# First batch of a fused attention and expert kernel: row products of two pairs of heads in two passes, memory cleared elsewhere, new slot tables

## The reference

```python
x = x + xattn(_layernorm(x), ctx, ctx, ...)          # stage A, first half
n1 = _ln(_layernorm(x), ln1_g, ln1_b)                 # stage A, second half
q, kk, v = n1 @ wq + bq, n1 @ wk + bk, n1 @ wv + bv   # two blocks, 16 heads, 16 columns a head
attn = softmax(q @ kk.T / sqrt(16)); ctx = attn @ v   # 512 x 512 scores for each of 32 heads
x = x + mix(ctx @ wo)                                 # stage C
x = x + sum over top 2 experts of gate * (gelu(n2 @ fw1[e]) @ fw2[e])
```

## Time and profile before

| | |
|---|---|
| median of 3 runs | 1400.85 us |
| lowest, highest | 1398.68, 1401.18 us |
| the profiled execution, its own time | 1400.36 us |
| its span in the trace | 1398.6 us |
| PE, DVE, ACT, POOL busy | 1353.3, 1090.8, 885.8, 371.5 us |
| mean granted TensorE clock | 0.994 |

### The profile page before, as it was taken

How to read it: one execution, slowest core, us unless ns; L and a number is a source line. 1 busy time by engine, 2 the same in 40 slices (tenths; PEclk the granted TensorE clock), 3 DMA queues, 4 the chain that set the end, 5 groups by cost and what they waited for, 6 DMA issues and landing times.

```text
span 1398.6 us, 25195 instructions
## 1 busy us (share of the span) xinstructions
PE 1353.3 (97%) x8671; PEld 639.5 (46%) x8672; DVE 1090.8 (78%) x2368; ACT 885.8 (63%) x1693; POOL 371.5 (27%) x360
## 2 busy tenths in 40 slices
PE   7889999999999999999999999999999999999999
PEld 4633433455344543445444453445434454443356
DVE  6769987978789777987779787897879877787621
ACT  3256667775677656775577756776567755756751
POOL 8613151113413033223142133130332231330000
PEclk9999999999999999999999999999999999999999
DMA  4013012211311213211132103112131211212002
GB/s 118 17 46 99 24 58 88 77 54 31 107 66 66 69 39 114 76 62 47 46 114 77 54 31 106 63 70 69 39 114 69 68 48 46 84 47 69 17 1 90
DMA packets 90711, 90.34 MB, mean 65 GB/s; under 512 B 14880, under 2 KB 85664, under 8 KB 89692
## 3 DMA queue, kind: packets, MB, share of 16 engines
q1 hardware_dynamic: 90588, 88.73, 19.3%
HBM read 35.05 MB, written 4.25 MB: 28 GB/s over the span
## 4 chain that ended last, share of the span: by engine, by line
PE 79%; issue 8%; DVE 6%; ACT 5%; POOL 1%; DVEq 0%; ACTq 0%; POOLq 0%
PE psum L913 15%; PE psum L930 13%; PE psum L744 8%; PE psum L881 8%; PE psum L897 7%; PE psum L862 7%; PE psum L500 6%; PE psum L529 4%; DVE mx L1433 3%; PE psum L779 2%; ACT prob L1745 2%; PE psum L617 2%; PE psum L590 1%; PE psum L627 1%; PE psum L505 1%
## 5 line engine op out<-in xcount | busy, mean ns | idle before, releaser
L1745 ACT ACTIVATE prob<-psum 128x512 f32<-128x512 f32 x1024 | 555.3, 605 | 314.3 <-PE psum L930 206.4
L1433 DVE TENSOR_REDUCE mx<-psum 128x1 f32<-128x512 f32 x1024 | 642.6, 681 | 81.0 <-PE psum L897 78.7
L913 PE MATMUL psum<-qst,kst 64*128 64x512 bf16 x2048 | 296.2, 379 | 7.0 <-ACT prob L1745 3.8
L930 PE MATMUL psum<-prob,vst 128*17 128x512 f32 x2048 | 246.0, 595 | 0.6 <-ACT prob L1745 0.2
L897 PE MATMUL psum<-kst,qst 64*128 64x512 bf16 x1024 | 184.3, 379 | 9.9 <-DVE mx L1433 4.0
L913 PEld LDWEIGHTS psum<-qst,kst 64*128 64x128 bf16 x2048 | 75.8, 95 | 184.2 <-issue 136.4
L1896 POOL CAST parts<-resid 128x512 bf16<-128x512 f32 x64 | 40.8, 638 | 326.0 <-DVE resid L1304 326.0
L897 PEld LDWEIGHTS psum<-kst,qst 64*128 64x128 bf16 x1024 | 53.0, 93 | 142.6 <-issue 94.9
L881 PE MATMUL psum<-w,cxT 128*128 128x256 f32 x448 | 110.3, 393 | 0.0
L862 PE MATMUL psum<-n2T,x 128*128 128x512 f32 x224 | 103.2, 603 | 0.0
L930 PEld LDWEIGHTS psum<-prob,vst 128*17 128x17 f32 x2048 | 46.1, 96 | 122.4 <-issue 92.9
(11 more groups left out here) (251 smaller groups left out, 1703.2 us busy)
## 6 DMA issues: line engine op xcount, KB each, us to landing
kst<-parts SPq DMA_DIRECT2D x186, 128.0 KB, 2.1
qst<-parts SPq DMA_DIRECT2D x186, 128.0 KB, 2.1
cmat<-G_dram SPq DMA_DIRECT2D x7, 1024.0 KB, 4.6
x<-in_L_ffn_fw SPq DMA_DIRECT2D x14, 512.0 KB, 3.7
w<-in_L_ffn_fw SPq DMA_DIRECT2D x14, 512.0 KB, 3.8
xbuf<-in_x SPq DMA_DIRECT2D x8, 512.0 KB, 4.9
kin<-in_ctx SPq DMA_DIRECT2D x8, 512.0 KB, 4.0
out<-acc SPq DMA_DIRECT2D x7, 512.0 KB, 3.2
```

The costliest lines, as they stand in the source:

```text
L913: ins = e.matmul(psum[:, u.bank, :], kst[own, i, h // 2, g * P:(g + 1) * P], qst[own, i, h // 2, :], start=i == 0, stop=i == 1)
L930: ins = e.matmul(psum[32 * j:32 * j + VW, VB, :], vst[:, g, h, :], prob[:, g % 2, j, :], start=g == 0, stop=g == NT - 1, tile_position=(0, ...
L1433: e.tensor_reduce(mx[:, qq, par, j, t:t + 1], psum[:, u.bank, :], AX, ALU.max).then_inc(u.free, 1)
L1745: e.activation(prob[:, g % 2, j, :], psum[:, u.bank, :], ACT.Exp).then_inc(u.free, 1)
```

## The change

Five edits belong to the head of the program.

- The layers 1 of `kst` and `qst` are cleared only behind the first four head pairs (12 of 16 blocks), both by DVE: `kst` behind the gate columns, `qst` between `lf` and `F`. POOL clears only `chosen`.
- The products for pairs 0 and 1 go in two passes: first layer 0 of both (`pick_first`, high and middle part), later layer 1 (`pick_low`, high and low part), behind the third maximum tile.
- POOL makes both middle parts before both low parts.
- The projection of piece 2 (`p2`) moves from behind the last maximum's tiles to the slot of the last one. Pairs 2 and 3 come later between the maxima.
- `warm_clock(6)` becomes `keep_clock(4)`: four products of 256 columns in float32 in place of six of 512 columns in a one-pass format.

The slot tables of all three kinds of period are new. Only a few of their rows are shown.

```diff
-            PE_A=slots(-8, "kT0:4 kT1:0 qT0:0 qT1:0 gates:3 gsum:22 ...
+            PE_A=slots(-8, "kT0:4 kT1:0 qT0:0 qT1:0 gates:4 gsum:22 ...
...
-        HEAD = defaultdict(lambda: -9, p0=-7, s0=-7, p1=-6, s1=-6, pick2=3, pick3=9, p2=TILES, mean=TILES,
+        HEAD = defaultdict(lambda: -9, p0=-7, s0=-7, p1=-6, s1=-6, low=5, pick2=9, pick3=11, p2=TILES - 1, mean=TILES,
                            logits=TILES + 1, mexp=TILES + 1, s2=TILES + 1)
...
                         pick_first()
+                        yield "low"
+                        pick_low()
                         for h in range(PAIRS, HP):
                             yield f"pick{h}"
-                            pick([(which, j, h) for which in range(2) for j in range(3)])
+                            for which in range(2):
+                                for i in range(2):
+                                    pick(which, h, i)
...
             def pick_first():
 
-                for which, h in ((0, 0), (1, 0), (0, 1), (1, 1)):
-                    for j, made in enumerate((split_hi, split_mid, split_lo)):
-                        e.wait_ge(made, which + 1)
-                        pick([(which, j, h)])
+                for h in range(PAIRS):
+                    for which in range(2):
+                        e.wait_ge(split_hi, which + 1)
+                        e.wait_ge(split_mid, which + 1)
+                        pick(which, h, 0)
+
+            def pick_low():
+
+                for h in range(PAIRS):
+                    for which in range(2):
+                        e.wait_ge(split_lo, which + 1)
+                        pick(which, h, 1)
...
-            warm_clock(6)
+            keep_clock(4)
...
                 e.scalar_tensor_tensor(out=lf, in0=gf, scalar=0.0, in1=ga, op0=ALU.min, op1=ALU.subtract
                                        ).then_inc(va.here("lf", b), 1)
+                if b == 0:
+                    e.memset(qst[:, 1, HP:], 0.0).then_inc(ones, 1)
                 yield "F"
...
                     ins.then_inc(gate_setup, 1)
+                e.memset(kst[:, 1, HP:], 0.0).then_inc(ones, 1)
...
             e.memset(mrow[:], 1.0).then_inc(ones, 1)
-            e.memset(kst[:, 1], 0.0).then_inc(ones, 1)
...
                     yield f"s{n}"
-                    middle_low(b, n)
+                    if b == 0 and n < 2:
+                        middle(b, n)
+                        for k in range(2 if n else 0):
+                            low_part(b, k)
+                    else:
+                        middle_low(b, n)
...
             e.memset(vst[:, :, :, KD:KD + 1], 1.0).then_inc(consts, 1)
-            e.memset(qst[:, 1], 0.0)
             e.memset(chosen, 0.0).then_inc(choice_made, 1)
```

More of the change, by code:

```diff
@@ L370, in build @@
[L370 to L374 removed]
+            PE_A=slots(4, "kT0:2 kT1:3 qT0:2 qT1:0 gates:2 gsum:16 cols:17 cd0 cd1:0 st0:2 st1:0 st2:6 num0:3 num1:5 "
+                          "num2:0 num3:20 n1T0:0 n1T1:2 p0:5 p1:2 p2:9 p3:0 pv0:26 pv1:0 logits"),
@@ new lines, in build @@
+            ACT_S=slots(5, "p4:2 p5:16 p6:0 p7:14 v0:17 v1"),
+            POOL_A=slots(5, "pw:21 vcopy:10 mask0:9 mask1:3 mask2:0 mask3:0 vw:16 hw:11 hs:18 hn:0 x2:22 r1 r5:0 s0:0 "
+                            "s1:0 s2:9 s3"),
+            POOL_C=slots(22, "acc0:0 r1"),
+            POOL_S=slots(19, "s4:2 s5:6 s6:25 s7"),
+            SP_A=slots(-1, "ctx:0 x:2 gi:21 G:65 s0:3 s1:17 s2 s3"),
+            SP_C=slots(56, "w10:0 w20:7 w11:11 w21:24 out"),
+            SP_S=slots(-1, "s4:2 s5:24 s6:26 s7"),
@@ L505, in keep_clock @@
                     e.matmul(psum[:, VB, 0:2 * P], ident[:], ident[:].unsqueeze(1).to_broadcast([P, 2, P]), start=True,
-                             stop=True)
-            def warm_clock(n):
-                for _ in range(n):
-                    e.matmul(psum[:, VB, 0:4 * P], identR, identR.unsqueeze(1).to_broadcast([P, 4, P]), start=True,
                              stop=True)
@@ L679, in router, with pick @@
                 logits(u, mbc, rw, M)
-            def pick(order):
-                for which, j, h in order:
-                    for i in range(2):
-                        if j not in PARTS[i]:
-                            continue
-                        u = uses["pick", which, h, i] if j else take("pick", which, h, i)
-                        ins = e.matmul(psum[:, u.bank, :], chosen[:, which, i, PARTS[i].index(j), h, :], parts[:, which, j, :],
-                                       start=j == 0, stop=j > 0)
-                        if j:
-                            ins.then_inc(u.full, 1)
-            def pick_first():
-                for which, h in ((0, 0), (1, 0), (0, 1), (1, 1)):
-                    for j, made in enumerate((split_hi, split_mid, split_lo)):
-                        e.wait_ge(made, which + 1)
-                        pick([(which, j, h)])
+            def pick(which, h, i):
+                u = take("pick", which, h, i)
+                for n, j in enumerate(PARTS[i]):
+                    ins = e.matmul(psum[:, u.bank, :], chosen[:, which, i, PARTS[i].index(j), h, :], parts[:, which, j, :],
+                                   start=n == 0, stop=n == 1)
+                ins.then_inc(u.full, 1)
+            def pick_first():
+                for h in range(PAIRS):
[8 more added lines that the diff above has]
+                        pick(which, h, 1)
             def spread_G(b, h):
@@ L891, in maximum @@
                     for which in range(2):
-                        for i in range(2):
-                            w = uses["pick", which, h // 2, i]
-                            e.wait_ge(w.free, w.n)
+                        w = uses["pick", which, h // 2, 0]
+                        e.wait_ge(w.free, w.n)
                 for par, u in enumerate([take("max", b, qq, j, t, par) for par in range(2)]):
@@ L908, in score @@
                     e.wait_ge(rows_in[q_ % 2], 16 * (q_ // 2 + 1))
+                if b == 0 and h < HC and g == 0:
+                    for which in range(2):
+                        w = uses["pick", which, h // 2, 1]
+                        e.wait_ge(w.free, w.n)
                 us = [take("score", b, qq, g, 2 * j + par) for par in range(2)]
@@ L1194, in stage_a @@
                     residue(b, n)
-                for i in range(0 if b else 2):
-                    u = uses["pick", 1, 0, i]
+                if b == 0:
+                    u = uses["pick", 1, 0, 0]
                     e.wait_ge(u.full, u.n)
-                    e.tensor_copy(qst[:, i, 0, :], psum[:, u.bank, :]).then_inc(u.free, 1)
+                    e.tensor_copy(qst[:, 0, 0, :], psum[:, u.bank, :]).then_inc(u.free, 1)
                 yield "mean"
@@ L1888, in first_half, with middle @@
                 spread(b, slice(NG // 2, NG), 1)
-            def middle_low(b, n):
-                m, which, c = PIECES[n]
+            def middle(b, n):
                 q_, u = b * len(PIECES) + n, uses["proj", b, n]
@@ L1899, in middle_low @@
                                 ).then_inc(split_lo, 1)
+            def middle_low(b, n):
+                middle(b, n)
+                low_part(b, n)
             def second_half(b):
```

122 lines of the change are left out of this document (59 added, 63 removed), and 12 rows, old and new, of the table DVE_A.

## The result

| | before | changed |
|---|---|---|
| median, of 13 runs each | 1400.98 us | 1405.39 us |
| lowest, highest | 1398.68, 1402.99 us | 1402.7, 1407.6 us |
| ratio of the changed to before | | 1.003, 95% interval 1.0022 to 1.0039 |
| the profiled execution, its own time | 1400.36 us | 1406.88 us |
| its span | 1398.6 us | 1405.2 us |

The account below looks back on a forecast made before the run. TensorE, with work in flight for 97% of the span, was taken as the bound. Start -2.0, picks -1.5 and last maximum to first score -4.5 gave -8.0 us: 1392.9 us on the median's scale, range 1387.8 to 1397.6.

Parts of the forecast that it names:

- The lock on the port: Start: without POOL's qst memset blocking DVE's variance line, the first gate product moves from 12.83 to at most 8.8: 4.0 us.
- The clock of the gate products: Start: with little idle time in front, the gate products' 3.25 us pair may run at 2.4 GHz: 1.3 us won.
- The rival on the clock: Start: idle time before the first transpositions grows to 2.4 us, clock falls; start -0.3, total 1394.6 us; chance 0.15 within forecast's.
- The memset between `lf` and `F`: Start: DVE's new qst memset delays F, g, G and M, with nothing hiding it: 2.6 us lost.
- I charge 0.7 for both risks: Start: 0.7 us off the 2.7 us gain at G, for POOL's key-weight folding and a TensorE clock drop behind G.
- POOL's fold: Start: POOL folds the key weights until 29.8 us, unmoved by the change; a gain above 2.9 us would be cut off.
- The picks: Head: POOL's earlier middle part lets DVE's sixteen reductions start 2.1 us earlier; taken as -1.5 us, bounds 0.5 and 2.4.
- From the last maximum to the first score: Head: p2 and the gate sum leave this stretch, and the clock is fuller: -4.5 us, bounds 3.3 and 6.
- The first period: 91.6 to 242 us: 11.5 us open, but the trace doesn't say which order wins them: 0, with +-2 us.
- The middle periods: Six periods with 1.1 us each open to reordering: 0 with a fraction of that, so 163.5 us each.
- the late fourth pair behind `make_x3`: Middle periods: POOL's late parts make TensorE wait behind one maximum each; at 2 us each, 1404.9 us; chance 0.04.
- single pieces shifted by a few slots: Slot tables: changes move single pieces slightly; maxima placed by any slot differ by one at most in first and middle tables.

Follow-up runs that it names:

- the late clearing: Changed kernel with the qst memset behind M instead of between lf and F: 1400.67 us, ratio 1.0011; with all three old tables too, 1393.57 us, ratio 0.9949.
- 26 filling products: Changed kernel's head with all three old tables and keep_clock(26) instead of keep_clock(20) ahead of TensorE's wait for G: 1393.13 us, ratio 0.9953.
- the version with the lowest time: Changed kernel's head with qst cleared behind M, new first table, middle and last tables of before: 1390.73 us, ratio 0.9941.

## Why the prediction was wrong

By its own steps, each against what the profiles measured. The forecast was -8.0 us; the spans gave +6.6. The difference of 14.6 is 3.9 at the start, 0.9 at the picks, -0.3 at the first score, 1.4 in the first period, 2.65 in the middle ones, 1.1 from there to the ending and 5.0 in it.

- **The lock on the port, 4.0 us at the first gate product: right.** 12.83 became 8.78, at the late end of what was forecast. The memset of `kst` cost nothing, as taken: `lf` still waited 0.30 us for ScalarE behind it.
- **The clock of the gate products, 1.3: right.** L715's four took 1.91 instead of 3.25 us. Not always, though: in two other profiles with this head they took 2.84 and 3.06. The rival on the clock had put the four `keep_clock` products at 1.8 us by rows at the full clock; they took 3.78, and the first transpositions 0.6 more than before. So a part of that rival came true, but not by the growing idle time that it named.
- **The memset between `lf` and `F`, 2.6: right** in itself (2.62), and so was G at 25.4.
- **"I charge 0.7 for both risks": this step failed.** The clock drop behind G cost 10.28 - 5.58 = 4.7 us, where the forecast had 0.7 for it and POOL's fold together. The row that should have warned was in the argument itself: in the earlier trace rows TensorE is idle, and then at half the clock, behind about 1.5 us of idle time, and I had found that the change would put 2.6 us of nothing in front of G. Given that, the drop was the likely case, and not a risk to be weighed at a third. I had also priced the stretch at three and a half microseconds; it lasted ten, nearly all of the work that stands there: 5.6 us of it at the full clock became 10.3. The runs with the late clearing and with 26 filling products settle it: in both the stretch takes 5.55 us again, and with the old tables 4.5 and 3.9 us of the time come back. The first of these takes away the memset's delay too, the second the drop alone. The bound that POOL's fold was to set, 2.9 us, didn't hold either: with the late clearing the decay products start 5.5 us earlier than before (28.18 against 33.68), and TensorE then waits 0.30 us for POOL.
- **The picks, 1.5: too large.** The first reduction came 2.0 us earlier against the decay products, as argued. But the two gaps between the sixteen are 0.39 + 0.87 = 1.26 us, where I had put the bound at 0.9 and taken less, so that 0.6 is left.
- **From the last maximum to the first score, 4.5: right**, 4.8. The clock in it was 0.50 before, from 82 to 86 us, and is 1.00 in the changed kernel.
- **The first period, 0 with +-2: inside its bounds.** Up to the decay products of batch 2, 1.4 of the 3.5 us are given back. I had taken the gate sum's move for free. It cost a wait of 2.15 us for ScalarE's copy. But with it back in front of the scores the kernel was no faster.
- **The middle periods, 0 "with a fraction of 1.1 us each": this failed.** Against 163.05 us with the old middle table behind the same head, the new one takes 0.77 us more in each, and once 0.5 more: 4.4 us over five by the profiles, 3.8 for the whole by the ratios. Against the kernel before only 2.65 show, since four of its own five contained a stall of 0.4 us that is gone from the changed one (see the last section). The rival that I named, the late fourth pair behind `make_x3`, is not it: no wait for its rows shows. Nor are the two more table loads. No single wait of the period answers for the 0.77 us: TensorE has 1.1 us more in flight, and no group of its products stands out. So what makes the middle table slower stays open. Its rows were not put back one by one; only ScalarE's row of the gelus was tried apart.
- **The ending was not in the forecast at all.** I counted the edits of the last table as "single pieces shifted by a few slots", and didn't look which work each slot had in front of a wait. One of them took away the eight products that filled TensorE's time until DVE was done. By the ratios the last table costs 2.9 us, by the spans up to 5.0. The 2.9 is the better figure: over all profiles the ending takes 42.4 to 45.3 us with the eight products behind the mean, and 40.4 to 42.4 with the old last table. The eight products' own share is seen in the profile of one run only (45.3 against 40.65 us) and not in its median.

The forecast of 1392.9 is not far from what the new head can do: 1394.3 on the scale of 1400.85 us with the clock held by filling products, 1392.6 with the memset behind M and the first table new. The second is in part luck, since it also has the 2.8 us of the memset's delay, which the forecast had rightly charged. Within the changed kernel the first score came 3.5 us earlier; with the 4.7 of the drop added that would be 8.2, an estimate, against a forecast of 8.0. The head's gains were sized well. What went wrong was a gap in front of TensorE that was priced as a delay, and three tables that were priced by how far they move things, two of which cost time.

The Trainium skill (TensorE: Matmul & The Clock Gate, HAM oscillation) describes this pattern, a wait after which the engine starts again at the low clock. The trace agrees in the pattern, with 1.2 GHz behind waits of 2.64 and 2.21 us. It differs in one point: the page's rule warns only of longer idle gaps than these.

## What to carry to other kernels

Wherever a change makes TensorE wait for two microseconds or more, price the work behind the gap at 1.2 GHz too, not only the gap: behind waits of 2.15 to 2.64 us it ran at half the clock for three to ten microseconds here. Behind waits of 0.75 and 1.24 us at G it kept the full clock, but 1.5 us in one place and 0.49 us ahead of sixteen products of one column were enough for a drop. Filling the gap with products that nobody reads, or moving a memset past the instruction that TensorE waits for, each bought back some four microseconds with the old tables. Read a slot table by asking, for each wait, which work now stands in front of it: one number cost 20 us by putting four gelus ahead of an exponent, and another left eight products behind a wait that they used to fill. ScalarE, busy for 69% of a period, took two more table loads in each for nothing.

## What the runs showed of the hardware

**A period's length hung on ten nanoseconds.** With the same instructions in the same order, a middle period takes 163.05 or 163.49 us. Both occur in the run with 26 filling products. Its timelines of DVE, POOL and TensorE at the end of two of its middle periods, the longer one first:

```profile
440.54 0.67 DVE L1444 COPY mxx<-mx 128x32 f32<-128x32 f32 x1
...
440.54 1.23 POOL L1828 TENSOR_SCALAR_AFFINE_SELECT cmat<-cmat 128x512 f32<-128x512 f32 x2
...
441.36 0.27 PE L499 MATMUL psum<-ident,mxx 128*32 128x128 f32 x1 [0.79 <-DVE mxx L1444]
```
```profile
604.03 0.18 DVE L1444 COPY mxx<-mx 128x32 f32<-128x32 f32 x1
...
604.04 1.25 POOL L1828 TENSOR_SCALAR_AFFINE_SELECT cmat<-cmat 128x512 f32<-128x512 f32 x2
...
604.36 0.27 PE L499 MATMUL psum<-ident,mxx 128*32 128x128 f32 x1 [0.30 <-DVE mxx L1444]
```

Where DVE's copy of 32 elements starts 10 ns ahead of POOL's select, it takes 0.18 us; where both start in the same hundredth of a microsecond, 0.67, about as long as one of POOL's two selects (1.23 us together), and TensorE waits 0.5 us longer. By the Trainium skill (SBUF — State Buffer, Who interferes with whom) a copy can take the shared ports and whoever is first keeps them for its whole instruction; the rows agree. The kernel before had the longer form in four of its five lengths and the shorter (163.03 us) in one. In the changed kernel the copy takes 0.18 us, since POOL's selects are done before it. With the old tables and the new head it was the shorter form in all five, with the late memset besides the longer, and in the version with the lowest time the shorter. In each of these periods the copy took 0.67 us where the length was the longer one and 0.18 where it was the shorter; the lengths differ by 0.4 us. That was read from the profiles and not tested by an edit of its own. It means that some 2 us of any comparison here can come from where a change happens to put these two instructions.

**The clock behind the same 0.49 us of waiting** stays low for different times. At the ending, with the old last table, the same instructions from L833 to the end of the span take 40.4 us in the kernel before, with 26 filling products and in the version with the lowest time, and 42.0 to 42.4 us in three others. The clock is low for some 3.4 us in the first three and for some 6.8 in the others. Why isn't known; it is a spread of 2 us in single executions.
